# A graph layer on one core: edge tiles of 128 rows in place of 125, ids turned on the chip, and a small memset behind every gather

## The reference, cut to what matters

```
xn = layernorm(x)
# graph attention
el, er = per-node logits (8 heads) from xn;  feat_v = xn @ W_val + b_val
e   = leaky_relu(el[src] + er[dst])
a   = softmax of e over the edges of each dst
gnn = segment_sum(feat_v[src] * a, dst)
# linear attention ("the mixer") over all nodes
Q, K, V = xn @ Wq, xn @ Wk, xn @ Wv
phi(v)  = max(exp(-0.5 |v|^2), eps) * exp(min(v @ omega, 50))
mix = phi(Q) (phi(K)^T V) / (phi(Q) sum phi(K)) @ Wo
x = x + gnn + mix
# sinkhorn gates, top-k routing to 8 experts, one 512x512 product for each, scattered back
x = x + ffn(layernorm(x))
```

## Time and profile before

| | |
|---|---|
| median of 3 runs | 3177.48 us (3176.93 to 3179.5) |
| profiled execution | 3169.73 us, its span 3167.7 us |
| TensorE / VectorE / ScalarE / GpSimd busy | 80% / 51% / 31% / 70% of the span |
| mean granted TensorE clock | 0.92 of full speed |
| logit gathers L554, 800 | first at 137.8 us, last at 1485.5 us (with 50 scatters among them) |
| value gathers L596, 800 | first at 1490.2 us, last at 2751.5 us |

### The profile page before, as it was taken

One profiled execution on the slowest core, in us unless ns is written; L12 is line 12 of the kernel. 1 busy time (PEld: TensorE's weight loads), 2 busy tenths in 40 slices (PEclk: granted clock), 3 DMA queues, 4 the chain that ended last, 5 costly groups with the idle time before them and its releaser, 6 DMA issues.

```text
span 3167.7 us, 47560 instructions
## 1 busy us (share of the span) xinstructions
PE 2547.4 (80%) x10463; PEld 1775.2 (56%) x10464; DVE 1620.6 (51%) x2963; ACT 992.5 (31%) x2564; POOL 2208.5 (70%) x1847
## 2 busy tenths in 40 slices
PE   6699999999999979941776777777788888824998
PEld 3377766667766644421554556666666666723443
DVE  6622222222222279986744555565666666767232
ACT  2322222222222200020544545554555556600111
POOL 6477777877777877787877777777777777500454
PEclk9899999999999999975799999998999999956999
DMA  6531111111111133321666677777777777630111
GB/s 162 143 81 30 29 29 30 32 29 29 29 29 29 24 118 115 115 57 24 164 173 175 178 184 182 179 183 175 188 189 195 192 194 200 174 110 0 45 52 39
DMA packets 276634, 341.25 MB, mean 108 GB/s; under 512 B 165456, under 2 KB 184631, under 8 KB 276451
## 3 DMA queue, kind: packets, MB, share of 16 engines
q0 software_dynamic: 218672, 227.51, 32.0%
q1 hardware_dynamic: 52093, 93.57, 9.4%
q10 hardware_dynamic: 5810, 19.52, 2.0%
HBM read 285.65 MB, written 55.25 MB: 108 GB/s over the span
## 4 chain that ended last, share of the span: by engine, by line
POOL 41%; issue 16%; PE 15%; DMA 14%; DVE 9%; DVEq 3%; POOLq 0%; ACT 0%
POOL R L554 31%; PE ps L642 14%; DMA R<-val_tab,src_i 13%; POOL R L596 8%; POOL er_starts L567 2%; DVEq L240 1%; DVEq L1469 1%; DVE work L1563 1%; DVE R L1469 1%; PE ps L939 1%; DVE work L1229 1%; PE ps L667 1%; DVE work L1239 0%; DVE R L1450 0%; DVE work L1509 0%
## 5 line engine op out<-in xcount | busy, mean ns | idle before, releaser
L642 PE MATMUL ps<-R,work 125*125 (+3 forms) x5240 | 1639.7, 467 | 254.5 <-DVE R L1469 229.9
L642 PEld LDWEIGHTS ps<-R,work 125*125 125x125 f32 (+2 forms) x5240 | 978.9, 194 | 821.1 <-issue 689.2
L554 POOL DMA_INDIRECT R<-el_tab,src_i x800 | 985.6, 1232 | 323.6 <-issue 284.1
L596 POOL DMA_INDIRECT R<-val_tab,src_i x800 | 979.2, 1224 | 284.9 <-issue 185.6
L1469 DVE TENSOR_TENSOR R<-R,ps (+1 forms) x800 | 520.5, 692 | 131.7 <-DVE ps L1458 125.8
L1119 ACT ACTIVATE work<-work 125x125 f32<-125x125 f32 x900 | 277.8, 309 | 492.3 <-PE ps L642 464.2
L642 PE MATMUL ps<-work,R 128*128 128x250 f32 x1600 | 359.1, 383 | 21.9 <-DMA work<-R 21.9
L1116 ACT ACTIVATE work<-work,negdst 125x125 f32<-125x125 f32 x900 | 353.6, 393 | 73.9 <-issue 52.0
L642 PEld LDWEIGHTS ps<-work,R 128*128 128x128 f32 x1600 | 308.6, 194 | 59.1 <-issue 22.0
L1458 DVE COPY ps<-R (+1 forms) x401 | 69.7, 174 | 306.7 <-POOLq L602 233.1
L1301 DVE TENSOR_TENSOR R<-ps,R 125x512 f32<-125x512 f32 x50 | 34.6, 691 | 357.6 <-PE ps L642 357.6
(11 more groups left out here) (256 smaller groups left out, 2173.5 us busy)
## 6 DMA issues: line engine op xcount, KB each, us to landing
R<-el_tab,src_i POOLq DMA_INDIRECT x800
R<-val_tab,src_i POOLq DMA_INDIRECT x800, 6.0
val_tab<-R SPq DMA_DIRECT2D x50, 253.9 KB
work<-R SPq DMA_DIRECT2D x25, 500.0 KB, 3.6
work<-xm_tab SPq DMA_DIRECT2D x50, 250.0 KB
out_dram<-R SPq DMA_DIRECT2D x50, 250.0 KB
work<-in_x_dram SPq DMA_DIRECT2D x17, 500.0 KB
xm_tab<-work ACTq DMA_DIRECT2D x17, 500.0 KB
```

The costliest lines, as they stand in the source:

```text
L554: eng.indirect_dma_start(out=ELP[:, g, c, :], out_offset=None, in_=el_tab[:, :], in_offset=bass.IndirectOffsetOnAxis(ap=src_i[:, t:t + 1], ...
L596: eng.indirect_dma_start(out=ring[:, slot, :], out_offset=None, in_=val_tab[:, :], in_offset=bass.IndirectOffsetOnAxis(ap=src_i[:, 2 * u + ...
L642: return pe.matmul(o, l, r, start=start, stop=stop)
```

## The change

- **Edge tiles of 128 rows.** R = 128 gives TIL = 782 tiles in place of 800, still 13 blocks (CT = 49 columns of up to 16 tiles). All edge arrays grow to 128 partitions.
- **Ids turned on the chip.** The ids are loaded as rows and turned by TensorE transposes at the start of the norm stage. Destinations take one turn; sources take two, with a trip through a DRAM array `src_flat` between them.
- **A memset behind each gather.** After each of the 782 logit gathers and 782 value gathers GpSimd writes zeros into `pause`, 128 rows by 64 columns, under `Steps.done`.
- **The mixer.** TensorE does the plain values before the graph's values in `values(j)`, and a quarter of the queries between the two score products. VectorE's two-step "max, then multiply" of phi becomes one `scalar_tensor_tensor`, for keys (L1312, L1314) and queries (L1325, L1326).
- **Smaller parts.** The negated ids are made by ScalarE early; er is kept in an array of its own; VectorE waits for the el stores before it writes the ones of `vout4`.

```diff
+R = 128
+TIL = 2 * -(-E // (2 * R))
+CT = -(-TIL // NCH)
+LAST = TIL - (NCH - 1) * CT
...
+        pause = sb("pause", [128, 64])
...
+            eng.dma_start(id_col.bitcast(INT32), srcT).then_inc(S["ids_loaded"], 16)
+            load_x(0)
+            eng.wait_ge(S["ids_made"], 1)
+            eng.dma_start(id_dst[:, 0:TG, :].bitcast(INT32), spread_rows(dst, R)).then_inc(S["ids_loaded"], 16)
...
-            eng.dma_start(src_i[:, :], srcT).then_inc(S["idx_loaded"], 16)
             eng.wait_ge(S["row_ready"], 2)
             eng.wait_ge(S["el_written"], 16 * G)
-            eng.wait_ge(S["idx_loaded"], 16)
+            eng.wait_ge(S["ids_made"], 7)
...
                         eng.indirect_dma_start(out=ELP[:, g, c, :], out_offset=None, in_=el_tab[:, :],
                                                in_offset=bass.IndirectOffsetOnAxis(ap=src_i[:, t:t + 1], axis=0)).then_inc(logits_in[k % 2], 16)
+                        st.done(eng.memset(pause[:, :], 0.0))
...
                     eng.indirect_dma_start(out=ring[:, slot, :], out_offset=None, in_=val_tab[:, :],
                                            in_offset=bass.IndirectOffsetOnAxis(ap=src_i[:, 2 * u + s:2 * u + s + 1], axis=0))\
                         .then_inc(gathered[u % PAIRS], 16)
+                    st.done(eng.memset(pause[:, :], 0.0))
...
-            for u in range(ET // 2):
+            for u in range(TIL // 2):
...
                     if isinstance(g, int) and g == 1:
+                        turn_loaded_ids()
                         spread_params()
+                        turn_sources()
...
                 def values(j):
+                    pe.wait_ge(S["v_copied"], 2 * g + j)
+                    for k in range(KC):
+                        last = mm(ps[0:P, 3, :], xT[b][:, k, j * P:j * P + P], w_v[:, k, :], k == 0, k == KC - 1)
+                    last.then_inc(S["v_psum"], 1)
                     pe.wait_ge(S["vg_read"], 2 * g + j)
...
                 scores_k(0)
+                queries(0)
                 scores_k(1)
-                for c in range(C):
-                    for k in range(KC):
-                        last = mm(chunk(0, c, 0, GT), w_q[:, k, 128 * c:128 * c + 128], xT[b][:, k, :], k == 0, k == KC - 1)
+                for c in range(1, C):
+                    last = queries(c)
...
+            v.wait_ge(S["ids_loaded"], 64)
+            v.tensor_copy(id_col, id_col.bitcast(INT32)).then_inc(S["ids_made"], 1)
+            v.tensor_copy(id_dst, id_dst.bitcast(INT32)).then_inc(S["ids_made"], 1)
+            first_slot()
...
+            def keep_sources():
+                v.wait_ge(S["ids_turned"], 4)
+                v.tensor_copy(src_i[:, 0:512], ps[0:R, 0, :]).then_inc(S["ids_made"], 1)
+                v.tensor_copy(src_i[:, 512:TIL], ps[0:R, 1, 0:TIL - 512]).then_inc(S["ids_made"], 1)
...
-                    st.done(v.tensor_scalar(nk[0:P, j, :], nk[0:P, j, :], EPS_PHI, None, ALU.max))
...
-                    v.tensor_tensor(out=p3, in0=p3, in1=nk[0:P, j, :].unsqueeze(2).to_broadcast([P, H, F]), op=ALU.mult)\
-                        .then_inc(S["phi_ready"], 1)
+                    v.scalar_tensor_tensor(out=p3, in0=nk[0:P, j, :].unsqueeze(2).to_broadcast([P, H, F]), scalar=EPS_PHI, in1=p3,
+                                           op0=ALU.max, op1=ALU.mult).then_inc(S["phi_ready"], 1)
```

More of the change, by code:

```diff
@@ L22 @@
 NCH = 16
-CL = E // NCH
-CT = CL // P
+R = 128
+TIL = 2 * -(-E // (2 * R))
+CT = -(-TIL // NCH)
+LT = NCH * CT
+LAST = TIL - (NCH - 1) * CT
+CL = CT * R
+EP = NCH * CL
+LW = LT * 8
+assert TIL % 2 == 0 and 0 < LAST <= CT
+TG = TIL // 128
+TREM = TIL - 128 * TG
 X = 8
@@ L66, in block_tiles @@
 def block_tiles(k):
-    return NCH * (min(TB * k + TB, CT) - TB * k)
+    return sum(NCH if g < LAST else NCH - 1 for g in range(TB * k, min(TB * k + TB, CT)))
 def logits_by(k):
@@ L182, in gps_layer @@
         rcnt_ = rcnt[:, :]
[L183 to L187, removed]
+        EWLO = R2W - LW
+        EW = R2[0:R, EWLO:R2W].rearrange("p (t h) -> p t h", h=H)
+        EW2 = R2[0:R, EWLO:R2W].rearrange("p (u h) -> p u h", h=2 * H)
+        WS = [R2[:, LW + 2048 * i:LW + 2048 + 2048 * i].rearrange("p (k n) -> p k n", k=KC) for i in range(4)]
         w_vg, w_k, w_v, w_q = WS
@@ L521, in _ @@
             eng.sem_inc(S["consts_ready"], 1)
-            for t_ in (ident[:, :], halves[:, :], half2[:, :], before[:, :], EW2[:, ET // 2, :]):
+            for t_ in (ident[:, :], halves[:, :], half2[:, :], before[:, :]):
                 st.done(eng.memset(t_, 0.0))
@@ L551, in gather_logits @@
                 for g in range(TB * k, min(TB * k + TB, CT)):
-                    for c in range(NCH):
+                    for c in range(NCH if g < LAST else NCH - 1):
                         t = c * CT + g
@@ L608, in _ @@
                     report(u - BEHIND)
-            for u in range(ET // 2 - BEHIND, ET // 2):
+            for u in range(TIL // 2 - BEHIND, TIL // 2):
                 report(u)
@@ L642, in mm, with turn_ids @@
                 return pe.matmul(o, l, r, start=start, stop=stop)
-            pe.wait_ge(S["node_ready"], 1)
-            pe.wait_ge(S["tops_below"], 1)
+            def turn_ids(out_rows, tab, n, b):
+                for k in range(TG + 1):
+                    w_ = min(128, n - 128 * k)
+                    o_ = ps[0:out_rows, b + k // 4, (k % 4) * 128:(k % 4) * 128 + w_]
+                    last = pe.transpose(o_, tab[0:w_, k, :], ident[0:w_, 0:w_])
+                return last
+            pe.wait_ge(S["consts_ready"], 2)
+            pe.wait_ge(S["tables_ready"], 1)
+            pe.wait_ge(S["ids_made"], 3)
             for c in range(TC):
@@ L819, in turn_block @@
                 for g in range(TB * k, min(TB * k + TB, CT)):
[L820 to L821 removed]
+                    last = pe.transpose(ps[:, b, (g % TB) * R:(g % TB) * R + R], tab_[:, g - first, :, :].rearrange("p c h -> p (c h)"),
+                                        ident[0:R, 0:R])
                 last.then_inc(S["seg_t_psum"], 1)
@@ L1007, in trip @@
                         load_x(g + NXI, b)
+                    if isinstance(g, int) and g == 1:
+                        keep_ids()
                     if not isinstance(g, int) or g >= 1:
```

215 lines of the change are left out of this document (132 added, 83 removed).

## The result

The changed kernel takes 3952.06 us (median of 4 runs, 3937.3 to 3963.7) against 3178.49 for the kernel before beside it: ratio 1.2418, 95% interval 1.2359 to 1.2477. The forecast was 3500, range 2930 to 3600: the sign is right, the size is not, and neither is the reason.

The account below looks back on a forecast made before the run. GpSimd's gather list was taken as the bound, so the gathers' beat decides. Norm +4, logit stage +149 and value stage +170 gave +323 us on 3169.7: 3493, forecast 3500 for the runs' median, range 2930 to 3600.

Parts of the forecast that it names:

- the sign: Whole kernel: slower expected with chance 0.70, faster 0.26, same 0.04.
- the mixer's: Mixer step: savings there lie beside GpSimd's list and are worth nothing, with VectorE having 28.5 us to spare.
- The gap after a memset: GpSimd, before each gather: empty list expected to show 0.5 us of idle time instead of 0.30.
- the second rival: Gap after a memset stays 0.30 us; 3281 us, or 3187 with a logit beat of 1.52; chance 0.21.
- the third rival: Memset and wait hide inside the 0.30 us gap before a gather; beat 1.32 us, total 2947; chance 0.20.
- The width: GpSimd's gathers: 128 rows cost 1.02 us each, against 1.20 for 125 rows.
- the first rival: A gather of 128 rows costs what 125 cost, 1.20 us; total 3782; chance 0.07.
- The beats: Time per tile: logit stage 1.73 us against 1.505 (+149 us), value stage 1.81 us (+170 us).
- The terms per gather: Logit beat: memset start 0.05, memset 0.15, then 1.71 from memset to gather end, less 0.18 for the shorter gather.
- The norm: Norm stage: added conversions, copies and transposes put 4 us on the path, with bounds 0 to 10.
- The mixer's new order: Mixer: fills TensorE's two idle places per group, 40 us if GpSimd were out of the way.
- The fused maxima: VectorE in the mixer: take away 0.7 us and less each, counted as worth nothing beside GpSimd's list.

Follow-up runs that it names:

- e1: Changed kernel without its 1,564 memsets; 4149.6 us.
- e4: Changed kernel with four memsets, each waited for, behind each logit gather; value stage unchanged; 3596.9 us.
- e7: Changed kernel with logit gathers of 112 rows and no memset behind them; value memsets stay; 4124.6 us.
- e9: Changed kernel with logit gathers of 16 rows and no memset behind them; value memsets stay; 4125.9 us.
- e10: Changed kernel with logit gathers of 121 rows and no memset behind them; value memsets stay; 4107.3 us.
- e3: Changed kernel with logit gathers of 125 rows, all memsets kept; 3373.8 us.
- e16: Changed kernel without memsets and with the mixer's code of the kernel before; 2950.5 us.
- e17: Changed kernel without memsets and with semaphores numbered as in the kernel before; 2890.8 us.
- e6: Changed kernel with one and two memsets in turn behind the logit gathers; 3186.2 us.
- e18b: e17's kernel, unchanged, in another session; 4162.0 us, ratio 1.3047 to the kernel before.
- e14: Changed kernel with e6's logit memsets; value pairs with two waited memsets between, four unwaited of 16 columns behind; 3048.7 us, ratio 0.9619 to the kernel before.

## Why the prediction was wrong

**The step that failed** is the mixer's: "All of it lies beside GpSimd's list and is worth nothing here." It took for granted that the mixer's pace does not depend on how fast GpSimd issues. In sessions 0 to 3 and 6 it does: every kernel with logit gathers 1.39 us or less apart was slowed, and every one at 1.50 or more was not, whatever the rows; e1 and e4, of one session, differ by the memsets alone. The mixer's end, 1893 us, not the logit list's, 1322, then set the start of the value stage: 717.8 of the 794 us. The kernel before, at 1.505, sat just above that limit, which its profile cannot show.

**The sign was luck.** The forecast expected GpSimd's list to become longer. Counted at GpSimd alone it changed by -165 us in the logit stage and +77 in the value stage; what made the kernel slower is a stall that the prediction did not name, neither as a rival nor as a price.

**The gap after a memset** was the second failure, the one named as most likely. It was put at 0.5 us from the earlier trace rows and is 0.27; the second rival had it, and the beat of 1.39 lies between its 1.52 and the third rival's 1.32. The Trainium skill's figure (DMA: Bandwidth & Descriptors, "Anatomy of one DMA"), some 50 ns of sequencer time for a GpSimd DMA, pointed the right way: the list being empty costs nothing that can be seen here (0.27 us of gap against 0.30). No run takes the sequencer's part out of the 0.27. Those places of the earlier trace rows were wakings by another engine, or behind a wait for arrivals, not by GpSimd's own memset. In the value stage such waits do stand before the first gather of a pair, at 0.86 us; the forecast had 0.16 for both gathers of the pair in addition, and 0.59 is what they cost (0.86 less 0.27).

**The width** had the right direction and nearly the right size: 0.95 us where 1.02 was forecast and the first rival had 1.20. The line through 0.857 and 0.995 was drawn to a 112-row price with a bounds check; a 112-row gather without one takes 0.94 (e7). The timelines of e9, e7, e10 and e3 give, where the gathers are not at 1.40 us, 0.85 us for 16 rows, 0.94 for 112, 1.02 for 121 and 1.22 for 125. The Trainium skill's rule (the same page, "Why a DMA increments its semaphore by 16 and not by 1") splits over the largest divisor up to 16: 16, 16, 11 and 5. The measured lengths order themselves by it, and the packets in the traces count it: 12,512 of 256 bytes in the changed kernel (782 gathers, 16 shares of 8 rows), 8,602 of 352 bytes in e10 (11 shares of 11 rows), 3,910 more of 800 bytes in e3 than in the changed kernel (5 shares of 25 rows).

**The beats** were forecast at 1.73 and 1.81 us and are 1.39 and 1.69. The logit list ends 165 us earlier than in the kernel before (1321.9 against 1486.7), and the forecast had it some 150 later; the value list is +77 where +170 was forecast. The terms per gather are 0.95 for 1.02, 0.00 for 0.05, 0.17 for 0.15 and 0.27 for 0.51. The memset (0.17 for 0.15) and the 782 gathers were right; it starts with the gather's end and not 0.05 later. The norm cost 4.3 us (first logit gather 137.75, then 142.04) for a forecast of 4, but with the same code in that stage the first gather comes between 138.3 and 144.7 us in the runs, so the agreement says little.

**The mixer's new order** was put at 40 us if GpSimd were out of the way. e16 against e17, in one session and without memsets: division 1137 and 1080, totals 2950.5 and 2890.8, so 57 and 60 us (the numbers of the semaphores differ as well). The fused maxima, left at nothing, are in that too. In e3 to e6 it is the same 53 to 58 us against the kernel before, and there it is hidden behind GpSimd's list, as was said.

**The value stage** at 1.69 a tile is GpSimd's own list (391 pairs of 3.37 us are 1318): with the same code it takes 1338 to 1341 us in four sessions, all of the slowed kind. Without memsets it takes 1054 (e17) or 1346 to 1355 (e1, e18b), by the session.

What the changed kernel would take in a session like 5 was not run. An estimate from rows: its logit list ends at 1322, before the value stage can start (1394.5 in e17), then 1339.9 and 413.9: 3150 us, close to the kernel before and far from the forecast. There the memsets are pure cost, by this estimate 260 us against e17; where gathers stall the others they save about 160 at the mixer's end (1893 in session 0 against 2051 in session 1).

**Left open:** what in the device differs between the sessions, and what the gathers take from the other engines. Neither bytes nor rows nor DMA share is it (e9). Whether the kernel before would be slowed at 1.25 us in a session of the slowed kind was not run either. Whether e14 keeps its 3.8% in a session of the other kind was not run; its logit pace does (e6), its value gathers come as close as 1.37 us to each other and may not.

## What to carry to other kernels

Before you make a queue of small DMAs faster, ask what the other engines need while it runs, and look at their instruction counts by stretch and not only at the queue's own beat. When two unrelated undoings both cure a slowdown, doubt the comparison and run one of them again elsewhere before you build a theory on either. Look inside one execution for a stretch without the suspect, as the scatters are here. A kernel whose best case lies just past such a limit should be judged by its time in several sessions.

## What the runs showed of the hardware that was not expected

- GpSimd gathers 1.39 us apart or closer can leave TensorE with 1.2 matmuls a microsecond (after, beside the gathers) or 0.4 to 0.5 (e1, e7, e9, e10, e18b), where e17 has 4.4, at a DMA share of 0.04 to 0.10. Every kernel at such a pace was slowed in five sessions (0 to 3 and 6) and none in two (4 and 5); for one kernel both were seen (e17, e18b). It sets in between 1.39 and 1.50 us (at 1.445 it costs the mixer 20 us, in session 3).
- The granted clock was 0.59 to 0.68 from 200 to 1075 us in these kernels, mostly at the lower level (1.2 GHz), with TensorE idle for over half of the time, so the matmuls that did come were slower too (in e1 0.58 us for 0.43). Beside the scatters of e18b, with TensorE busy throughout, it was 1.00.
- A memset that GpSimd waits for leaves a gap of 0.27 us before the next gather, less than the 0.30 between two gathers that follow directly; unwaited ones leave 0.16.
